# Graph features and a top-2 expert layer on one core: 17 full expert tiles moved ahead of the last block's routing

## The reference, cut to what matters

```python
h2 = tanh(layernorm(x) @ W_proj + b_proj)
filt = tanh(adj * adj)                  # of each row the 350 largest are kept
x = x + relu(keep_350(filt) @ (h2 @ W_gcn) + b_gcn)

xn = layernorm(x)
scores = xn @ Wg.T + bg                 # 8 experts
top2, idx = top_k(scores, 2); p = softmax(top2)
x = x + sum over the two experts e of a row: p_e * (relu(xn @ W1[e].T + b1[e]) @ W2[e].T + b2[e])
```

## Time and profile before

| | |
|---|---|
| median of 3 runs | 513.22 us (513.01 to 513.41) |
| the profiled execution, its own time | 511.21 us |
| its span in the trace | 509.4 us |
| PE busy | 410.6 us (81%) |
| DVE busy | 370.3 us (73%) |
| ACT busy | 338.9 us (67%) |
| POOL busy | 247.0 us (48%) |

### The profile page before, as it was taken

The page is one execution under the profiler, slowest core; times in us unless marked ns, Lnnn a source line. Parts: engine busy times, 40 slices in busy tenths (PEclk is TensorE's granted clock), DMA queues, the critical chain, the costliest instruction groups (busy, mean ns, idle before and its releaser), DMA issues.

```text
span 509.4 us, 8989 instructions
## 1 busy us (share of the span) xinstructions
PE 410.6 (81%) x2671; PEld 256.7 (50%) x2672; DVE 370.3 (73%) x889; ACT 338.9 (67%) x345; POOL 247.0 (48%) x355
## 2 busy tenths in 40 slices
PE   0799999999898899999749999410999898989900
PEld 0455444444443445544334444210899898988900
DVE  4978899989999996696769999751555555554526
ACT  1789999799979876999757798100466555554500
POOL 2059941005206738718615875551266656564620
PEclk9999999999999999999978999855899999998975
DMA  8649589786666677586544781013233223232149
GB/s 242 266 146 378 219 286 374 251 283 245 222 243 213 227 264 284 188 292 272 196 181 129 278 314 69 31 43 121 77 88 96 82 62 92 64 86 65 40 155 339
DMA packets 31128, 95.56 MB, mean 188 GB/s; under 512 B 5532, under 2 KB 18132, under 8 KB 22896
## 3 DMA queue, kind: packets, MB, share of 16 engines
q1 hardware_dynamic: 19904, 80.06, 45.3%
q0 software_dynamic: 6048, 12.72, 7.5%
q10 hardware_dynamic: 5136, 2.30, 1.6%
HBM read 83.28 MB, written 12.67 MB: 188 GB/s over the span
## 4 chain that ended last, share of the span: by engine, by line
PE 21%; DVE 13%; issue 7%; DMA 4%; POOL 3%; SPq 2%; ACT 0%; POOLq 0%; DVEq 0%
DVE marks L820 5%; PE bank L1379 3%; PE bank L1380 3%; PE bank L1381 3%; PE bank L1400 3%; PE bank L1402 3%; PE bank L1401 3%; DMA tbuf<-expert_rows 2%; POOL expert_rows L602 2%; PE bank L1367 2%; POOL routed_rows L572 1%; DMA routed_rows<-aug,slots 1%; PE bank L1243 1%; SPq L422 1%; PE bank L1389 1%
## 5 line engine op out<-in xcount | busy, mean ns | idle before, releaser
L1269 PE MATMUL bank<-tbuf,g_sb 128*128 128x512 f32 x512 | 232.6, 602 | 1.7 <-ACT g_sb L1036 1.4
L1269 PEld LDWEIGHTS bank<-tbuf,g_sb 128*128 128x128 f32 x512 | 94.8, 192 | 108.9 <-issue 101.1
L820 DVE SCALAR_TENSOR_TENSOR marks<-abuf,marks 128x2048 bf16<-128x2048 int32 x56 | 128.3, 2291 | 1.2
L1016 ACT ACTIVATE tbuf<-abuf 128x2048 f32<-128x2048 f32 x64 | 121.4, 1897 | 3.5 <-PE bank L1269 2.7
L1020 ACT ACTIVATE tbuf<-tbuf 128x2048 f32<-128x2048 f32 x64 | 122.3, 1910 | 2.0
L602 POOL DMA_INDIRECT expert_rows<-abuf x78 | 76.7, 983 | 65.2 <-ACT abuf L1136 37.8
L572 POOL DMA_INDIRECT routed_rows<-aug,slots x64 | 83.7, 1308 | 50.4 <-DVE base L798 31.6
L982 DVE SCALAR_TENSOR_TENSOR tbuf<-bank,tbuf 128x512 f16<-128x512 f32 x78 | 51.8, 690 | 34.4 <-ACT tbuf L1130 34.4
L1130 ACT ACTIVATE tbuf<-bank 128x512 f16<-128x512 f32 x78 | 46.5, 597 | 44.5 <-PE bank L1381 43.1
L1400 PE MATMUL bank<-w2h,tbuf 128*128 x312 | 54.5, 220 | 0.0
L1401 PE MATMUL bank<-w2l,tbuf 128*128 x312 | 54.5, 220 | 0.0
(11 more groups left out here) (222 smaller groups left out, 510.8 us busy)
## 6 DMA issues: line engine op xcount, KB each, us to landing
abuf<-in_adj_tiles SPq DMA_DIRECT2D x64, 1024.0 KB, 5.2
abuf<-routed_rows SPq DMA_DIRECT2D x41, 130.0 KB, 2.1
wstage<-in_w POOLq DMA_DIRECT2D x16, 256.0 KB, 7.0
tbuf<-expert_rows SPq DMA_DIRECT2D x8, 512.0 KB, 6.9
out<-xres ACTq DMA_DIRECT2D x8, 256.0 KB, 6.2
expert_rows<-abuf POOLq DMA_INDIRECT x78
routed_rows<-pad SPq DMA_DIRECT2D x9, 130.0 KB, 2.5
routed_rows<-aug,slots POOLq DMA_INDIRECT x64
```

The source lines that it names most:

```text
L820: dve.scalar_tensor_tensor(mark, bits_in, 1.0, mark, ALU.min, ALU.add).then_inc(s_raw, 1)
L1016: act.activation(tbuf[:, n % NBUF, :, :], abuf[:, n % NBUF, :, :], ACT.Square).then_inc(s_sq, 1)
L1269: last = pe.matmul(ps_feat[ib % 2][:, :], g_sb[:, c, :], tbuf[:, buf, cc, :], start=(c == 0), stop=(c == C - 1))
```

## The change: what it does

- The stream loop has 65 steps (`FFN`), and behind it come `read_redo` and the expert tiles. The last block's routing (steps 65 to 71) is called from inside the tile iterations: `route_steps(FFN + t)` in iteration t, ahead of `turn_x(t+2)` on PE, behind `copy_x` on DVE, behind `y_out` on ACT.
- At step 58 (`FIRST`) DVE makes a first table (`first_tiles`) of the full tiles of the first six blocks in routing order, of which there are at least 17 (`N1`), signal `s_first`. Tiles 0 to 16 use it. SP loads them when the scatters of those six blocks have landed. The 22 others come from a second table (`last_tiles`) that DVE makes in iteration 7.
- SP's 8 pads come behind the load of tile 12; tile 17 waits for the pads, for all scatters and for `s_tab`. POOL's scatter of the last block comes behind the stores of tile 5.
- PSUM is shared out anew: `ps_xt` and `ps_y` have one bank instead of two each, and the last block routes in banks 5 and 7. `hh`, `hl` and `xhl` lie at the start of `tbuf`.
- `F0` is 23, so 16 tiles run in the loop (two passes).
- In the stream's last steps the marks of chunks 62 and 63 come one step earlier, the counts of the last block and the flags come in step 63, and PE's matmul of the flags stands between the second and third group of chunk 63.
- At the start `x` comes in three pieces (4, 8 and 20 column groups of 128 rows) instead of two (12 and 20); ACT and PE wait for the weights later and take the first group through before the second.

```diff
-    PIECES = [(0, 3 * CK), (3 * CK, C)]
+    PIECES = [(0, CK), (CK, 3 * CK), (3 * CK, C)]
-    F0 = 15
+    F0 = 23
+    SIX = NB - 2
+    N1 = (2 * SIX * IW - E * (TS - 1) + TS - 1) // TS
+    PADS = 12
+    LAST_SCATTER = 5
+    FFN = NCH + 1
-    END = START[-1] + 10
+    END = START[-1] + AT_ASSIGN + 1
+    FIRST = START[SIX - 1] + LATER[SIX - 1] + AT_ASSIGN + 1
...
+        in_stream, in_tiles = Space(ps_x2, ps_xn, bank[6]), Space(bank[5], bank[7], bank[7])
+        def space(i):
+            return in_tiles if i == NB - 1 else in_stream
-        ps_xt = [bank[4 + q][:, 0:TS].bitcast(fp16) for q in range(2)]
+        ps_xt = bank[4][:, 0:TS].bitcast(fp16)
+        ps_y = bank[6][:, 0:2 * D]
...
@@ SP
             load_x(0)
+            load_x(1)
...
                 if n == 0:
-                    load_x(1)
+                    load_x(2)
...
+            def pad_rows():
+                sp.wait_ge(s_padr, 1)
+                for e in range(E):
...
+            sp.wait_ge(s_sq, NCH)
+            sp.wait_ge(s_raw, NCH)
+            for i in range(2):
+                sp.wait_ge(routed.scat[i], SIX // 2 * Q * 16)
+            sp.wait_ge(s_first, 1)
+            for t in range(N1):
+                if t >= NX:
+                    sp.wait_ge(s_sc[t % NX], t // NX * 32)
+                load_tile(t, t % NX, first_r)
+                if t == PADS:
+                    pad_rows()
             sp.wait_ge(s_pads, 16 * (E + 1))
             for i in range(2):
                 sp.wait_ge(routed.scat[i], NB // 2 * Q * 16)
             sp.wait_ge(s_tab, 1)
+            for t in range(N1, F0):
+                sp.wait_ge(s_sc[t % NX], t // NX * 32)
                 load_tile(t, t % NX)
@@ POOL
-            scatter(NB - 1, routed)
             redo = read_redo(pool)
...
             for t in range(F0):
                 store_tile(t, t % NX, loop=False)
+                if t == LAST_SCATTER:
+                    scatter(NB - 1, routed)
@@ DVE
+            def first_tiles():
+                count_tiles(-0.5 + 0.5 / TS)
+                link(dve.tensor_tensor_scan(ends[:, :], ones_f[0:1, 0:E], tiles[:, :], 0.0, ALU.mult, ALU.add))
+                link(dve.tensor_tensor(used[:, 0:E], tiles[:, :], ends[:, :], ALU.subtract))
+                link(dve.tensor_scalar(used[:, 0:E], used[:, 0:E], float(N1), 0.0, ALU.add, ALU.max))
+                link(dve.tensor_tensor(used[:, 0:E], used[:, 0:E], tiles[:, :], ALU.min))
+                dve.memset(used[:, E:E + 1], 0.0)
+                link(dve.tensor_scalar(skip[:, :], tiles[:, :], -float(TS), float(RS), ALU.mult, ALU.add))
+                find_tiles(first_e, first_r, False).then_inc(s_first, 1)
...
-            for n in range(END):
-                if n < NCH:
-                    mark_positive(n)
+            for n in range(FFN):
+                for m in range(NCH):
+                    if n == (m if m < NCH - 2 else m - 1):
+                        mark_positive(m)
+                if n == NCH - 1:
+                    counts_out(NB - 1)
+                    flag_rows()
...
+                route_steps(n)
+                if n == FIRST:
+                    first_tiles()
+                if n == NCH - 1:
+                    decide_redo()
...
             for t in range(F0):
                 cut_h(t, t % 2)
                 copy_x(t + 2, t % 2)
+                route_steps(FFN + t)
+                if FFN + t == END:
+                    last_tiles()
@@ ACT
-            act.wait_ge(s_w, 64)
-            act.activation(ex[:, 0:1], bp_sb[:, 0:1], ACT.Tanh)
+            act.wait_ge(s_ident, 1)
+            act.activation(ex[:, 0:1], ident[:, 0:1], ACT.Tanh)
+            turned_out(0)
             square_chunk(0)
+            act.wait_ge(s_w, 64)
+            projected_out(0)
             tanh_chunk(0)
-            turned_out(0)
+            gcn_out(0)
             turned_out(1)
-            projected_out(0)
-            turned_out(2)
-            projected_out(1)
-            gcn_out(0)
@@ PE
             turn_group(0)
+            pe.wait_ge(s_w, 64)
+            project(0)
+            gcn(0)
             turn_group(1)
-            project(0)
-            turn_group(2)
-            project(1)
-            gcn(0)
...
+                    if n == NCH - 1 and cc == CK // 2:
+                        pe.wait_ge(s_flagged, 1)
+                        pe.matmul(ps_flag, ones_bf[:, :], flagged[:, :], start=True, stop=True).then_inc(s_nflags, 1)
...
+                if n == NCH - 1:
+                    block_counts(NB - 1)
...
+                route_steps(n)
                 if n < NCH:
                     chunk_features(n)
+                if n == 0:
+                    project(1)
+                    turn_group(2)
...
             for t in range(F0):
+                route_steps(FFN + t)
                 pe.wait_ge(s_xl[(t + 2) % NX], ((t + 2) // NX + 1) * 16)
-                turn_x(t + 2, (t + 2) % NX, t % 2)
+                turn_x(t + 2, (t + 2) % NX)
+                if t + 1 == N1:
+                    pe.wait_ge(s_tab, 1)
...
```

More of the change, by code:

```diff
@@ L313, in gnn_moe_layer @@
         s_padr = sem("s_padr")
+        s_first = sem("s_first")
         s_tab = sem("s_tab")
@@ L428, in _ @@
             sp.wait_ge(s_tab, 1)
[L430 to L438, removed]
+            sp.sem_inc(s_spare, 1)
+            for t in range(N1, F0):
+                sp.wait_ge(s_sc[t % NX], t // NX * 32)
+                sp.sem_inc(s_spare, 1)
                 load_tile(t, t % NX)
@@ L589, in _ @@
                     scatter(i - 1, routed)
-            scatter(NB - 1, routed)
             redo = read_redo(pool)
             with pool.If(redo > 0):
-                for b in range(NB):
-                    scatter(b, rerouted)
+                for i in range(NB - 1):
+                    scatter(i, rerouted)
             def store_tile(t, u, loop=True):
@@ new lines, in route_steps @@
+            def route_steps(n):
+                for i, b in enumerate(ORDER):
+                    if n == START[i] + AT_ADD:
+                        add_features(i, b, routed, scale=(i >= POOLED))
+                    if n == START[i] + LATER[i] + AT_NORM:
+                        normalise(i, b, routed)
+                        cut_rows(i, routed)
+                    if n == START[i] + LATER[i] + AT_CHOOSE:
+                        choose(i, b, routed)
+                    if n == START[i] + LATER[i] + AT_SECOND:
+                        choose_second(i, b, routed)
+                    if n == START[i] + LATER[i] + AT_PROB:
+                        probabilities(i, b, routed)
+                    if n == START[i] + LATER[i] + AT_ASSIGN:
+                        assign(i, routed)
@@ L939, in _ @@
                 dve.wait_ge(s_xre, 16)
-                for b in range(NB):
-                    add_features(b, b, rerouted, scale=True)
-                    normalise(b, b, rerouted)
-                    cut_rows(b, rerouted)
-                    choose(b, b, rerouted)
-                    choose_second(b, b, rerouted)
-                    probabilities(b, b, rerouted)
-                    assign(b, rerouted)
-                chain[:] = before_if
-            dve.tensor_copy(pad_i[:, :], base[0:1, :]).then_inc(s_padr, 1)
@@ L966, in _ @@
[L966 to L969 removed]
+                for i, b in enumerate(ORDER[:NB - 1]):
+                    add_features(i, b, rerouted, scale=True)
+                    normalise(i, b, rerouted)
+                    cut_rows(i, rerouted)
+                    choose(i, b, rerouted)
+                    choose_second(i, b, rerouted)
+                    probabilities(i, b, rerouted)
+                    assign(i, rerouted)
```

278 lines of the change are left out of this document (153 added, 125 removed).

## The result

The change took 497.62 us (median of 4 runs, 491.45 to 501.04) against 513.12 us (4 runs, 512.2 to 513.41), a ratio of 0.966 with a 95% interval of 0.9609 to 0.9712. Predicted were 495.0 us and a range of 487 to 503. The runs of the change lie 9.6 us apart, those of before 1.2 us; beside experiments 1 to 4, on another chip, twelve of the thirteen runs of the kernel before lie 8.2 us apart (510.77 to 518.99), so such a spread isn't peculiar to the change. The profiled execution is the longest of the four (501.04 us, a span of 498.9 against 509.4), so its sum shows 10.5 us of gain where the median shows 15.5.

The account below looks back on a forecast made before the run. PE bounds the tiles, and the stream is full; the 35.5 us join was what could shorten. Terms summed to -18.2 us on an execution of 511.2, giving 493.0; with 2.0 for the median, 495.0 us, range 487 to 503.

Parts of the forecast that it names:

- The start (-1.8): Start of the kernel: smaller first piece of x gives DVE a lead kept to the end, -1.8 us, bounds 0 and -5.
- The stream's end (+6.2): Last stream steps: DVE's first table, 4.3 us and not hidden, and the new order end PE's last chunk 6.2 us later.
- The join (-28.7): Between PE's last chunk and the first turned tile: 6.4 us instead of 35.1, so -28.7 us.
- The rival of a late branch: Join: a late branch leaves part of the 28.7 us there, each microsecond one lost; chance 0.01.
- The last block beside the tiles (+2.5, +4.3): First tile iterations: routing adds 2.5 us of PE work and 4.3 us of PE waits for DVE.
- One loop pass less (-1.8): Tile loop: one pause at the beginning of a loop pass goes, -1.8 us.
- The single banks (0): Tiles: one PSUM bank each for ps_xt and ps_y costs nothing.
- POOL and the buffers (+1.1): Tiles: the last block's scatter delays tile 14's load, +1.1 us; POOL's lag is gone before tile 38; bounds 0 and 7.
- Slow scatters: Tiles: the last block's scatters run slow, lag grows 6.5 us, 501.5 us; chance 0.16, including another wait on POOL's lag.
- The half clock: Tiles: at half clock the gain is gone from 7 tiles on, 19.6 us; 8 tiles give 517.4 us; chance 0.03.
- My sign of being wrong, the clock down in the tiles: Tiles: a clock down there was named among the signs that the prediction is wrong.
- The other side, fewer delays than I counted: Whole kernel: PE's 5 us lead survives and slack takes up DVE's delays, -3.2 - 4.3, so 487.5 us; chance 0.20.

Follow-up runs that it names:

- experiments 1 to 4: Four follow-up kernels on one chip, three variants of the changed kernel and one of the kernel before; the kernel before ran beside them at a median of 513.56 us.
- 1: Changed kernel with POOL's loads of weight pieces 8 and 9 issued ahead of its second bias work: 495.87 us, ratio 0.963 to the kernel before.
- 3: Kernel before with only the change's new start (x in three pieces, new order on ACT and PE): 514.75 us against 513.56, ratio 1.0008.
- 10 to 12: Changed kernel, third chip: weights early, first table late, F0 31; then also second bank and shared-out scatter; then also later scaling: 532.06, 531.02, 530.02 us.
- 4: Changed kernel with the first table moved from step 58 to behind the redo flag in step 63: 494.1 us, ratio 0.9635 to the kernel before.
- 5: Changed kernel with tile 1's turn in a second PSUM bank: one profiled run, span 495.8 us.
- 7: Changed kernel with the last block's eight scatter DMAs issued in pairs behind the stores of tiles 5 to 8: one profiled run, span 491.1 us.
- 2: Changed kernel with the start of the kernel before (x in two pieces, old order on ACT and PE): 494.71 us, ratio 0.9652 to the kernel before.
- 6: Changed kernel with the last block's scaling, and all that follows it, one tile iteration later: one profiled run, span 493.4 us.
- 9: Changed kernel as it is, again on another chip: 538.63 us against 541.62 for the kernel before, ratio 0.9932.

## Why the prediction was right, and where it was off

The forecast case came true: the join went, the stream's end and the tiles paid part of it back. The median is 2.6 us above the 495.0. That closeness is partly luck: the traced execution gained 10.5 us where 18.2 were predicted for one like it, with misses of +5.8, +1.0, -2.1, +2.6 and +0.4 us by stage, and no execution near the median was traced. Point by point:

- **The start (-1.8): the step that failed.** The marks came at 29.1 and PE at 17.9, as worked out, but the term counts DVE's lead as kept to the end. It took no account of what PE, 3.6 us early, would find at step 8: a weight piece that stands behind POOL's bias chain. In the profiled execution that made +4.0, outside the bounds of 0 and -5; with the piece early (1) a lead of 0.8 was left at chunk 57, and the new start by itself is worth nothing that can be measured (3, 1.0008, 0.9964 to 1.0052). Where POOL is out of PE's way, in 10 to 12, 2.2 to 2.6 us are left, so the size of 1.8 wasn't the fault.
- **The stream's end (+6.2): measured +7.2.** The table is on the path (4.80 us of wait, 4.2 us of work; without it +2.5, by 4). The flags were no wait. What I hadn't counted is the clock: it was down behind the wait, and chunk 61 took 2.2 us more.
- **The join (-28.7): measured -30.8.** The first tile was turned 4.3 us behind the last chunk instead of 6.4. I had given SP 3.9 us for the read and branch, and that was a wrong reading: in the kernel before SP was through them 1.0 us behind `redo_i`, at 339.17, and then waited 2.8 us for DVE's `pad_i`. Here SP's load was issued 2.1 us behind `redo_i`. PE's own branch took 3.75 us by its sequencer's records (3.88 before) and ended at 335.45, 0.4 us before the load landed at 335.82; SP's took 0.055 us. A quicker load would have met PE's branch next. The rival of a late branch is out.
- **The last block beside the tiles (+2.5, +4.3).** The two waits on the cut are right to 0.1 us (3.5 against 3.4), the one on the normalise is 0.3 instead of 0.9. The turns of tiles 5, 6, 8 and 11, where these steps stand, are 18.1 us behind the ones before them instead of 4 x 2.99 = 12.0: +6.1, against 6.8 predicted.
- **One loop pass less (-1.8): right.** Before, three pauses of 1.77, 1.90 and 1.94 us; now two, of 1.76 and 2.09.
- **The single banks (0).** At tile 1 the turn waited 1.12 us for the copy, when the clock was down behind the join; with a second bank tile 1's load was the next wait (5). On the other chip the other single bank has 20.7 us of waits.
- **POOL and the buffers (+1.1): +1.8,** spread over tiles 13, 14 and 15 instead of tile 14 alone. The lag was 9.4 us over its usual 3.0 (a scatter of 10.1 was predicted, and then a lag of under 7) and gone at tile 17, long before 38. Taking the scatter apart moved the wait on (7).
- **Not in my sum:** 1.2 us at tile 19 for reading the second table's experts, and the 1.7 us lost in the first tiles, at half clock.
- **The rivals.** Slow scatters fell: 0.96 us each. The half clock wasn't there while the last block was routed beside the tiles, but it was behind the join (0.51 from 336.0 to 342.8) and behind the second pause. My sign of being wrong, the clock down in the tiles, did show at these two places, but the kernel before has both as well (0.50 from 355.5 to 360.0, and 4.72 us for the tile behind its last pause), and the 1.7 us lost in the first tiles are far from the 19.6 that would have cost the gain. The other side, fewer delays than I counted, is not seen either. A chip on which the gain shrinks to 0.7% was in none of my cases.

The half clock is where several of these points meet. Waits of 3.96, 4.80 and 3.94 us each left PE at the 1.2 GHz level, and waits of 1.8 us on the cut didn't. In between the length of a wait doesn't tell: one of 1.90 us at the weights did (3), one of 1.64 didn't (2), of the two loop pauses (1.76 and 2.09) the second did, one of 2.5 us for a load didn't (6), and of two in the stream of the kernel before, 3.35 us at 252.9 left the clock at 1.00 and 3.48 us at 260.5 was followed by 0.62. The Trainium skill (TensorE: Matmul & The Clock Gate, Part 1: The HAM clock gate) says that half rate is the default and activity lifts it. The rows agree: after the wait of 4.80 us PE was busy without a gap from 316.9 on, at 0.51, and from 322.3 the clock was 1.00.

## What to carry to other kernels

A gain at the head of a pipeline counts only when every other queue that the earlier engine meets later is early as well: follow it to the next transfer it waits for, and to the engine that is busiest. Work put on a serial engine under a stream is hidden only if no other engine waits for what comes next from it; here PE already waited 0.76 us for DVE, the table's 4.2 us came on top, and the wait of 4.80 took the clock with it. Before a gap behind a branch is put down to the branch, look whether the engine was waiting for another one: SP's 3.9 us were 1.0 of its own and 2.8 of DVE's. Merging two PSUM banks into one takes away slack that hardly mattered in one trace, and in that of another chip the merged bank carried 20.7 us of waits; time such a change on more than one chip.

## What the runs showed of the hardware

- A wait of PE of about 4 us cost more than itself: chunks of 3.6 us took 5.8 (twice), the four transposes of the first tile 0.59 us instead of 0.39. Behind waits of 1.9 to 3.5 us the clock was sometimes down and sometimes not.
- The same not-taken `redo` branch took PE 3.3 to 3.9 us (3.88 before, 3.75 in the change, 3.53 in 4, 3.33 in 9) and SP 0.055 us each time, by the records of their sequencers. DVE's record in the kernel before is 0.07 us, but its next instruction started 2.8 us behind it.
- One chip ran the same tiles at 4.2 us instead of 2.99 at full granted clock, with ACT's `y_out` starting 1.7 us later against PE's turn, and yet ran the stream of the same program to within 0.6 us of the other chip at the start of every chunk but two (33 and 34, 1.9 us).
